# New order tables for the four engines and a new PSUM bank table in a two-layer transformer kernel

## The reference, cut to what matters

```
h = layernorm(x) * (1 + ca) + sa
x = x + ga * L0_attn(h)      # kernel-feature linear attention, 16 heads, then two norms and a 512-wide MLP
h = layernorm(x) * (1 + cb) + sb
x = x + gb * L0_ffn(h)       # 8 experts, top 1, low-rank updates
h = layernorm(x) * (1 + ca) + sa
x = x + ga * L1_attn(h)      # test-time-training attention: 16 heads, chunks of 64 tokens in sequence
h = layernorm(x) * (1 + cb) + sb
x = x + gb * L1_ffn(h)       # token-shifted, gated feed-forward
```

## Time and profile before

| | |
|---|---|
| median of three executions | 996.8 us (991.23 to 997.6) |
| profiled execution, its own time | 1000.52 us |
| its span, first to last instruction | 998.7 us |
| PE (matmul) busy | 935.8 us, 94% |
| VectorE busy | 793.1 us, 79% |
| ScalarE busy | 658.9 us, 66% |
| GpSimd busy | 332.4 us, 33% |
| mean granted TensorE clock | 0.965 of full |

### The profile page before, as it was taken

How to read it: one execution, slowest core, us unless ns; L and a number is a source line. 1 busy time by engine, 2 the same in 40 slices (tenths; PEclk the granted TensorE clock), 3 DMA queues, 4 the chain that set the end, 5 groups by cost and what they waited for, 6 DMA issues and landing times.

```text
span 998.7 us, 27045 instructions
## 1 busy us (share of the span) xinstructions
PE 935.8 (94%) x10914; PEld 711.8 (71%) x10914; DVE 793.1 (79%) x1953; ACT 658.9 (66%) x1246; POOL 332.4 (33%) x434
## 2 busy tenths in 40 slices
PE   6789899999999999899999999899999999999995
PEld 4566566686787776677777786688777786777773
DVE  3855549978988779997889869987888957888973
ACT  2363345788666576798766586699766566787772
POOL 1970002233341422234331331223441333455451
PEclk9689979999999999999999999999999988999998
DMA  9000010000000010000000010000000000000000
GB/s 327 16 2 1 1 43 2 2 2 2 2 1 3 12 44 1 2 2 2 2 13 1 12 44 1 2 2 2 3 12 2 12 12 12 1 4 12 2 2 21
DMA packets 15831, 16.03 MB, mean 16 GB/s; under 512 B 2013, under 2 KB 14301, under 8 KB 15325
## 3 DMA queue, kind: packets, MB, share of 16 engines
q1 hardware_dynamic: 15709, 14.31, 4.8%
HBM read 10.12 MB, written 2.10 MB: 12 GB/s over the span
## 4 chain that ended last, share of the span: by engine, by line
PE 64%; DVE 23%; ACT 5%; issue 3%; POOL 3%; DMA 1%; ACTq 0%; SPq 0%; DVEq 0%; POOLq 0%
PE ps L532 8%; PE ps L593 5%; PE ps L576 4%; PE ps L599 4%; PE ps L525 4%; PE ps L617 4%; PE ps L587 4%; PE ps L514 3%; PE ps L481 3%; PE ps L472 3%; PE ps L507 3%; DVE tmp L1122 2%; DVE tmp L1127 2%; DVE gbase L1128 2%; PE ps L398 2%
## 5 line engine op out<-in xcount | busy, mean ns | idle before, releaser
L1323 POOL TENSOR_TENSOR gbase<-zhat,gamma 128x512 f32<-128x512 f32 x64 | 81.6, 1275 | 320.7 <-DVE scl L1116 313.2
L1331 POOL TENSOR_TENSOR zq_sqq<-zq_sqq,qinv 128x512 f32<-128x512 f32 x64 | 67.9, 1062 | 260.3 <-DVE qinv L1139 254.0
L593 PEld LDWEIGHTS ps<-grad,k_sc 64*65 64x65 f32 x2048 | 67.9, 138 | 24.4 <-issue 22.4
L779 ACT COPY w_sb<-ps 65x1024 f32<-65x1024 f32 x66 | 66.4, 1006 | 24.3 <-PE ps L593 20.6
L532 PEld LDWEIGHTS ps<-w_sb,keys 65*64 65x64 f32 x2048 | 66.1, 139 | 20.6 <-issue 11.6
L593 PE MATMUL ps<-grad,k_sc 64*65 64x64 f32 x2048 | 75.9, 224 | 3.1 <-DVE grad L1133 2.8
L532 PE MATMUL ps<-w_sb,keys 65*64 65x64 f32 x2048 | 73.6, 225 | 5.2 <-ACT keys L787 3.6
L532 PEld LDWEIGHTS ps<-w_sb,queries 65*64 65x64 f32 x2048 | 65.1, 138 | 15.8 <-issue 7.9
L532 PE MATMUL ps<-w_sb,queries 65*64 65x64 f32 x2048 | 72.6, 224 | 3.2 <-DVE feats L1006 1.2
L599 PEld LDWEIGHTS ps<-h,pack_ttt 128*128 128x128 f32 x512 | 65.6, 198 | 12.4 <-issue 6.6
L599 PE MATMUL ps<-h,pack_ttt 128*128 128x128 f32 x512 | 72.1, 287 | 1.0 <-DVE feats L1006 0.7
(11 more groups left out here) (244 smaller groups left out, 2348.2 us busy)
## 6 DMA issues: line engine op xcount, KB each, us to landing
x<-in_x SPq DMA_DIRECT2D x8, 256.0 KB, 3.0
xc<-x SPq DMA_DIRECT2D x16, 128.0 KB, 2.4
out_x<-xc SPq DMA_DIRECT2D x16, 128.0 KB, 2.4
pack_ttt<-in_ttt SPq DMA_DIRECT2D x1, 1216.0 KB
keys<-in_gam_bet_rows SPq DMA_DIRECT2D x1, 1024.0 KB
w_sb<-in_compose SPq DMA_DIRECT2D x1, 1024.0 KB, 9.3
zq_sqq<-in_wmod SPq DMA_DIRECT2D x1, 768.0 KB, 5.6
pack_expert<-in_expert SPq DMA_DIRECT2D x1, 680.0 KB, 15.9
```

The lines of the kernel that those rows point to most:

```text
L593: last = mm(bank[2 * f + c][0:C, h * HD:(h + 1) * HD], k_sc[64 * c:64 * c + 64, HH * f + h, :], grad[64 * c:64 * c + 64, h, :], start=Fals ...
L779: nc.scalar.copy(w_sb[:, f, :, :, :].rearrange("p b h d -> p (b h d)"), ps[0:C, 2 * f:2 * f + 2, :].rearrange("p a c -> p (a c)")).then_in ...
L1323: P.tensor_tensor(gbase[:, cols], zhat[:, cols], gamma2[:, cols], ALU.mult).then_inc(S["g_hat"], 1)
L1331: P.tensor_tensor(heads(zq_hat[:, cols]), heads(zq_hat[:, cols]), per_head(qinv[:, hs]), ALU.mult).then_inc(S["zq_ready"], 1)
```

## The change

Only the strings change: all four of `ORDERS`, and `BANKS`. The number of steps of each kind is the same, as are all instructions, tiles, semaphores and transfers. As the change describes itself, the tables were made by a planner that lets a VectorE product with its inputs in SBUF and a GpSimd product exclude each other in time. The first string of each table line, as an example:

```diff
-    "PE": ("11001101101000111001101100101010011011100010010p0rks0lkqasl0b1qa010dkklbea1d1leabk1q0bdlfkefla0dqkqea10bolkff1bdoqaekl"
+    "PE": ("10101101010100101101101100101010011001110010010p0rkslqkab0ls0qa011k0dlbe1akdl1ekab1q0dbflkeal0fdqqae10kbokfl1fd1boqael"
...
-BANKS = ("0123456710234567314607321456073562071435620714356207143562071435620714356270143562701435674567456745747546754565746546"
+BANKS = ("0123456701234567031467205314631746205137462051374620513746205137462051374602513746025137465745675464654765457654764"
```

More of the change, by code:

```diff
@@ L110 @@
-    "POOL": ("zzzyyzzyyzzyyzzoyzyozyoozyzyzyzyozoyyyoozzzyzyzyyzzyozozyzyyzoyzozyyzyzyzyyyoooozzzyzyzyyzzyzozyoyzyzoyzoyzyzyzyzyooyy"
-             "ozozzzyyzyzyzyzoyzyzooyzzyyzoyzyzoyyzyyooo"),
-}
-BANKS = ("0123456710234567314607321456073562071435620714356207143562071435620714356270143562701435674567456745747546754565746546"
[L114 to L120, removed]
+    "PE": ("10101101010100101101101100101010011001110010010p0rkslqkab0ls0qa011k0dlbe1akdl1ekab1q0dbflkeal0fdqqae10kbokfl1fd1boqael"
+           "kd1eab01qq1l1fkbd0ea1ldb0fk0ead01qlbqok0feadb10lk1faedblo0kqf0am0ledbfqq0okea10mk0lq1fdb0ea0ldbfq01ea1omqfdb1e1fdoe1f0"
+           "fmo1m0rkkml1qbal0am0k10dlbk1laed1qmbake1d0blqqfaekdlqfaeq1k0blof10dfbak1eql1dmba1ek11qkd0bol1f0ad10lebkfqea0dlb0o0qfea"
+           "1q0kdbl1k0mfaedblo0fae0kfkqd0bolql0ea0q1mdbfk10eal0fqdb1ae1oq0md1fb1mdfee10offm1ormkkl1l0aa0b10kqql0db1mmeakdl1keb1maq"
+           "0dlbkqalfe0dqfeakbo1qflb1d0keqaf11lmbodk10ae1d1bkl1qf0ead10lfb0eak0obqdkl0qfea1bdkq0lf1oaedb0lm0fea0kbl1d1f0qkaedqo0ql"
+           "0kfe0lamb01qf1dbma1eo0fbqd1mdfee1of0m1kfrlmabkqlkoamqdblklaeqdbabeqmkkldbfaeqdflkbsaeokqmdflsbleafdmokaeqldbqfkmaebldq"
+           "fkaebodlkbqafedqflbkaeqdlokbafedpflkemsapqbdolqfakefldbqsmeaopqdbfefsmodefmfmsmommmm"),
@@ new lines @@
+    "ACT": ("1100110100010111011001110110000101111001000100p10r0ksl1kaqvls0qa0v1kdle01akvldewkav11wq0dlkfealvfdqqawewvk0ofl1f11dokq"
+            "ae0vdl1ewkaw1vqq10kfd0leavl0w1d0kefavdq11lqo0wk0afev1lkd01aevfwld0wkof0avqml0ef0dqokewqav0kw1mqfd0l10aev0ldfqw1eaw1oq0"
+            "vdf1me1fdweowsf0f1m1srokm10lakmvlq0ma0vk1dlk1lavdeq0a1kew1vd0lwqqafekvdlqfaweqvwk1lm0fodf11kaeq1lvdwm1eak1v00q1ok0ldwa"
+            "fv0delfke1aqwv10dlo00qfea1wvkqld010fwakewvldo0aefvkf0wq0kdolq00leamqwmvdf0keal101vfdq1aevwom1w1fqd01dfewews0s1ffo1mmom"
+            "r1k0kllava010vm0kqqld1maekv1ldke1awqv0ldwkqalevfdwqeafkwv11oqlf0d1mke1qfav0lmwdok1ave11001kdlfqwave0fdlw01eavko0qwkdlf"
+            "qa10veqkldf01aowvedw0lm0eavk0lfdfq0aekwdvqwo10q0lfke0lmav101fqdma1wm1eovwfdq01defwewsfo101mkrlfavmkskloaqvqdlkamevldaq"
+            "vewmkkldqfawveqwdlfkaevoqmwdkfllaevfdmwoakevqdlqkfwaevldfqkeavlwodkwqafvepdflqkaevqwdlkowafvedmflewpkaqvdowlmqfakveldw"
+            "fqaepmomwvdfefqowdefwmfommmmmm"),
@@ new lines @@
+    "DVE": ("101011010100100110111010110010011110011000101000r0101azbacz00bcaez11abezcyy0bcaez101aey0bycz1b0caze11eb1y1azc1bceya0z0"
+            "10byca0z1ebc0y1az0bceaezy0bca0ymzm001bec0ayze1010ybazc1e0mbcmeay01zbye1cy1e0y11mr01m10azmbcaz00bcaz1e1bcaezy1bycamze0y"
+            "ea1z0bcy101bc1ae101zbyca1ezbc01ayz010ebcayz10e0mbcaz0ybe0cyae1mzbmyca0ze000bc0eamyz1bcy1az1eb00ac1zye0bcym0mey1e1y111r"
+            "0m10azmabcz0m0bcaz1e1bcyaze0bycae0z1eayzb1yc11b0ma1cmz1ebc1ayz1b1ce0ya0z1eby0ca1ze00b0cazyb0e0cayz1emb0cyaz00bce1eya0z"
+            "m0y1a0bz1cm1becyaey0z0bc0me1mye1y11rmazbcazmbcazmebazcybecayzeybmaczeybcaezbcamyzebcayezmbcazebycayzebcazyebcayzebcyaz"
+            "embycazmebyceayzbceymeymmmmmmm"),
@@ new lines @@
+    "POOL": ("zzzzyyzyyzzyzyzyozozoyzyozyyzzoyyzyyyooozzzyzyzyyzzyzzyzoyzoyyozoyzyzyzyzooyyyoozzzyzyzyyzozyzyzyzzyooyzozyyzyzyyozyyo"
+             "ozozzzyyzyozyzoyzyzzyoyzzyoyzyzyozyyzyooyo"),
+}
+BANKS = ("0123456701234567031467205314631746205137462051374620513746205137462051374602513746025137465745675467464654765457654764"
+         "6754675745645647564756456746456474647646454654764574564564567456755764756746754676746547657465746576576457646576476576"
+         "5764756476546547654675674567546754756754547657465746547654765765746757546746767564756545764564576457564764764756475647"
+         "5675467567564756745764764765467467467467454657476547654764754657645745764574467546754656764654765474657467564754674645"
+         "7467547547546754745645647564756475675456745647564767467675647564757645645467546765746574674567456746467547645746547567"
+         "5465465746574657465746576475647564756754675654756457464756745674567456456457647647456457567546754765475476547645764764"
+         "5764576456745764657457456574754675467645674646546746745764647456746764756476546756465764756745764746765745475645754756"
+         "45754574657645647546576576457645764")
```

## The result

The changed kernel took 1028.1 us (median; 1024.6 to 1032.9) beside 997.2 us for the kernel before in the same runs: ratio 1.032 [1.026, 1.038], so some 32 us slower, where 991.0 us had been forecast (range 981 to 1002). The profiled execution has a span of 1022.5 us.

What follows compares the result with a forecast made beforehand. PE, busy 935.8 of 998.7 us, was taken to bound the kernel, leaving at most 62.9 us to win. The start's 5.4 us plus the pair start's 0.4 gave 5.8, so 991.0 us from the 996.8 median; range 981 to 1002.

Steps and rivals of the forecast that it cites:

- What bounds the kernel: Whole kernel: PE is busy 935.8 of 998.7 us, so 62.9 us is the most any order could win.
- The start: First 58 us: four reorderings let CONTEXT start 5.4 us earlier, bounds 3 to 8, and the gain is passed on.
- The first norm: In the start: ScalarE copies row 1 first, so QKV of row 1 waits less; 1.4 us gained, bounds 0.7 and 1.62.
- waits for Q_SHIFT: In the start: Q_SHIFT of row 0 goes ahead of L405, so VectorE's 1.76 us wait disappears; 1.8 us gained.
- ScalarE's copies: In the start: K_MAX of row 0 goes ahead of K_SHIFT of row 1, so VectorE's wait disappears; 1.0 us gained.
- K_SHIFT of row 0: In the start: STABLE of row 0 goes ahead of row 1's subtractions, so the 2.60 us wait shrinks; 1.2 us gained.
- The pair start: At 372 us: with zhat first, the mixing's norm lies under GpSimd's gbase; 0.4 us gained, bounds 0 and 1.37.
- The full stretches: From 430 to 590 us: PE has no idle time to give, so loss is possible, gain is not; 0.
- The port: VectorE and GpSimd products slowing each other, 9.3 us over two engines: mostly beyond the tables' reach; 0, bounds 0 and 4.
- The end: From GpSimd's last products on: PE and VectorE keep the same order; 0.
- C: Rival: steps put right behind a reply make engines wait, eight places at 2.2 us each; 1009 us, chance 0.12.
- B: Rival: keeping two-input products clear of the other engine's pays everywhere, 4 and 3 us more gained; 984 us, chance 0.24.

Runs made afterwards that it cites:

- head_of_after: The kernel before with only the first 49 steps of PE and ScalarE, 48 of VectorE and 85 bank entries of the changed kernel: 989.9 us, ratio 0.992.
- before_memset: The kernel before with GpSimd's three slot products replaced by memsets of about the same length, part of the computation left out: 991.0 us, ratio 0.994.
- after_memset: The changed kernel with GpSimd's three slot products replaced by memsets of about the same length, part of the computation left out: 979.5 us, ratio 0.984.
- after_z_last_memset: The changed kernel with 17 VectorE steps moved in front of `z` and GpSimd's three slot products replaced by memsets: 996.9 us, ratio 1.000.

## Why the prediction was wrong, point by point

- **What bounds the kernel**: right, but read too narrowly. PE's 62.9 idle us bound a gain. They bound no loss, and I used them as if they bounded both.
- **The start, 5.4 us**: right, in size and in its parts. From L362 to CONTEXT it took 40.97 us before and 34.46 after, 6.5 us less, inside 3 to 8. The first norm gained 1.5 (L362 to L373: 3.53 and 2.01 us; forecast 1.4). VectorE's waits for Q_SHIFT (1.76 us) and for ScalarE's copies (1.0) are gone, as forecast, and the 2.60 us for K_SHIFT of row 0 are 1.22, with 0.56 new for the transpose: 0.8 gained, 1.2 forecast. ScalarE's gap of 13.38 us before L723 is 5.40, so shorter but not gone. The gain was passed on: head_of_after took 8 us less than its partner. In the earlier trace rows PE had the lower clock for 23.9 us, mean 0.50; the same stretch of time (34.4 to 58.3 us) had 0.65 after.
- **The pair start, 0.4 us**: the step that failed first. "With zhat first, the norm lies under gbase" is right about the order (the 1.37 us wait did go) and names precisely what is blocked. The norm's price was taken from a row in which nothing overlapped it (1.11 us in the earlier trace rows); under two products it is 2.81. The place's alternative order is worth 1.0 us without blocking and costs 0.6 with it, and three such swaps cost 6 us of the kernel. Bounds of 0 to 1.37 took in no loss, although had a 128x6 step taking 1.01 us next to L1331. The rule quoted beside it is about two SBUF inputs, and L1165 has one; but the trace of before had a blocked step of L1165's kind too, LN2 of a row directly behind `y`, beside L1331 and the three output products that follow it. It took 2.67 us, where four L937 took 1.11 elsewhere:

```profile
263.53 2.67 DVE L937 TENSOR_SCALAR tiles<-y,mv,inv 128x128 f32<-128x128 f32 x4
263.60 1.04 POOL L1331 TENSOR_TENSOR zq_sqq<-zq_sqq,qinv 128x512 f32<-128x512 f32 x1 [5.67 <-DVE qinv L1139]
```

- **The full stretches, 0, "gain is not, loss is possible"**: the loss came, 2.2 us of idle PE in 160 where 0.7 had been. Two of the three pair starts lost some 2 us each, the third nothing (4.9 us of idle time from 800 to 860, 4.8 before), and 150 to 350 us, which the forecast left out, lost 5.6.
- **The port, 0 with bounds 0 to 4**: the step that decided. It was taken as a cost that can only shrink, where the new tables raised it from 6 to 48 us. It was sized from L1122, L1127 and L1326 of before, 9.3 us on two engines; before_memset shows 18.1 us of stretch on VectorE alone, for which that order pays 6 us. It cannot say what another order will pay, since of the steps that the new tables put under the products L1165, L992 and L993 stood nowhere under them before and carried no stretch in the old trace, and L937 hardly (the place above). "The tables can't reach" was wrong: they reach it by what stands directly behind `z`, and the count of those steps behind `z`, 0 before and 17 after, was in the order. At what one blocked place turned out to cost VectorE, 2.81 - 1.11 = 1.7 us for a norm (4 places) and 0.69 + 0.84 = 1.5 us for L992 and L993 (6 places), ten of the 17 make 16 of the 28 us by which VectorE's stretch grew.
- **The end, 0**: right within a microsecond. From this L1331 to the end of the span it took 33.3 us before and 34.1 after. L1170 beside L1331 again took 1.01 us, and ScalarE's last copy waited 2.43 us for PE (2.26 in the earlier trace rows):

```profile
988.42 1.30 POOL L1331 TENSOR_TENSOR zq_sqq<-zq_sqq,qinv 128x512 f32<-128x512 f32 x1 [4.59 <-DVE qinv L1139]
988.74 1.01 DVE L1170 TENSOR_TENSOR diff<-h 128x6 f32<-128x6 f32 x1
...
999.37 0.27 ACT L841 COPY att<-ps 128x128 f32<-128x128 f32 x1 [2.43 <-PE ps L617]
```

- **Rivals**: C had the right sign, with 12 us of loss where 32 were measured, and by another mechanism: the blocking made the producers late, and without it (after_memset) the new order is 12 us faster than the old one, so waits from the order alone don't make the loss. C's "from seven places on" is also a little low: 7 times 2.2 is 15.4 us, short of the 15.8 it has to use up. C's mechanism exists too, as after_z_last_memset showed (17 us for 17 moves). B had it backwards: the mean of L1122 fell by 8 ns, but those of L1127 and L1326 rose by 78 and 14. The chance of 0.11 for slower was too small for a change whose rule is about a cost the old trace shows only in part.

## What to carry to other kernels

A trace of before prices contention only where the old order lets it happen; a single long instance of a short instruction (L937's 1192 ns against a median of 341) is worth a look before it is averaged away. When a change reorders an engine's list, go through the new order and count what lands directly behind each step that releases the other engine's work, with the time of a blocked step, not a free one. And undoing such a placement by moving the trigger later is no remedy where the trigger's result is wanted: choose what stands behind it (the old order has `e`, a reduction, behind 20 of its 64 `z`, and pays 6 us in all), or, where the computation allows it, give the other engine work that doesn't read SBUF.
